# Relative attention with queries spread over heads by column multiplies, fp32 strips for Q·K, and row-wise probabilities written back as columns

## The reference

```
qx, kx, vx = split_head(x @ Wq.T), split_head(x @ Wk.T), split_head(x @ Wv.T)      # 16 heads of 8
ex   = rel_embed[ns].reshape(n, NH, HD).transpose(1, 0, 2)
srel = srel_skew(einsum('bhnd,hmd->bhnm', qx, ex))         # pad by one column, reshape, shift
qk   = (einsum('bhnd,bhmd->bhnm', qx, kx) + srel) * inv_dim
atten = softmax(qk - mask, axis=-1)                        # causal
out  = einsum('bhnm,bhmd->bhnd', atten, vx) ... @ Wp.T + bp
```

## Time and profile before

| | us |
|---|---|
| median of 3 runs | 4997.43 (4973.68 to 5001.73) |
| the profiled execution | 4969.21 |
| its span | 4967.5 |
| PE busy in the span | 4473.0 (90%), 30219 matmuls |
| DVE busy | 2379.6 (48%) |
| ACT busy | 1719.1 (35%) |
| POOL busy | 843.7 (17%) |
| mean granted PE clock | 0.912 of full speed |

### The profile page before, as it was taken

How to read it: one execution, slowest core, us unless ns; L and a number is a source line. 1 busy time by engine, 2 the same in 40 slices (tenths; PEclk the granted TensorE clock), 3 DMA queues, 4 the chain that set the end, 5 groups by cost and what they waited for, 6 DMA issues and landing times.

```text
span 4967.5 us, 76834 instructions
## 1 busy us (share of the span) xinstructions
PE 4473.0 (90%) x30219; PEld 2776.4 (56%) x30275; DVE 2379.6 (48%) x6906; ACT 1719.1 (35%) x3496; POOL 843.7 (17%) x1441
## 2 busy tenths in 40 slices
PE   7998989889898898988989889899898998989989
PEld 3556645565455654556545575455754457545575
DVE  3435634356443554435544355444554445544455
ACT  2322432325333343333433234333343333433334
POOL 2003110031100311103011040111401114011130
PEclk8989979999899998999989999899998999998989
DMA  2000000000000000000000000000000000000000
GB/s 68 1 1 1 1 6 1 1 1 1 6 1 1 1 1 6 1 1 1 1 6 1 1 1 1 6 1 1 2 1 6 1 1 2 1 3 1 1 1 3
DMA packets 19571, 17.25 MB, mean 3 GB/s; under 512 B 2462, under 2 KB 18799, under 8 KB 19183
## 3 DMA queue, kind: packets, MB, share of 16 engines
q1 hardware_dynamic: 19183, 11.99, 0.8%
HBM read 9.89 MB, written 2.10 MB: 2 GB/s over the span
## 4 chain that ended last, share of the span: by engine, by line
PE 80%; DVE 6%; POOL 6%; ACT 5%; issue 3%; DVEq 0%; ACTq 0%; POOLq 0%; SPq 0%
PE banks L984 7%; PE banks L974 7%; PE banks L988 7%; PE banks L880 7%; PE banks L908 6%; PE banks L825 6%; PE banks L920 3%; POOL work L478 3%; PE banks L865 3%; PE banks L1180 3%; PE banks L1201 2%; PE banks L1167 2%; PE banks L1074 2%; PE banks L1047 2%; PE banks L1023 2%
## 5 line engine op out<-in xcount | busy, mean ns | idle before, releaser
L1369 DVE CUSTOM_DVE_ANT_0 work<-banks,mask_row 128x512 f32<-128x512 f32 (+3 forms) x1024 | 451.6, 488 | 274.0 <-PE banks L880 270.6
L880 PE MATMUL banks<-work 32*128 32x512 f32 (+3 forms) x2048 | 526.7, 493 | 11.4 <-DVE work L1369 11.4
L908 PE MATMUL banks<-work 32*128 32x256 f32 (+3 forms) x2048 | 512.7, 504 | 20.8 <-ACT work L638 20.8
L638 ACT ACTIVATE work<-banks 128x384 f32<-128x384 f32 (+1 forms) x768 | 368.9, 526 | 441.9 <-PE banks L908 440.3
L437 POOL TENSOR_TENSOR rstd<-rstd,half 128x2 f32<-128x2 f32 x128 | 87.5, 703 | 2451.2 <-DVE moments L1297 1834.2
L654 ACT ACTIVATE work<-banks 128x512 f32<-128x512 f32 (+1 forms) x384 | 228.8, 596 | 687.6 <-PE banks L984 687.4
L1441 DVE TENSOR_TENSOR work<-work,banks 128x512 f32<-128x512 f32 (+1 forms) x384 | 263.5, 686 | 344.8 <-PE banks L988 344.5
L984 PE MATMUL banks<-xnT,wg 128*128 128x512 f32 (+1 forms) x768 | 417.8, 627 | 0.0
L988 PE MATMUL banks<-xnT,wu 128*128 128x512 f32 (+1 forms) x768 | 406.1, 611 | 0.0
L447 POOL TENSOR_SCALAR_AFFINE_SELECT work<-work 128x128 f32<-128x128 f32 (+1 forms) x768 | 252.6, 332 | 897.4 <-ACT work L638 886.1
L974 PEld LDWEIGHTS banks<-wd,work 128*128 128x128 f32 (+1 forms) x3072 | 360.6, 191 | 57.3 <-issue 57.3
(11 more groups left out here) (255 smaller groups left out, 7254.4 us busy)
## 6 DMA issues: line engine op xcount, KB each, us to landing
x_next<-in_L_attn_a_x_dram SPq DMA_DIRECT2D x8, 256.0 KB, 2.8
out_dram<-x SPq DMA_DIRECT2D x8, 256.0 KB, 2.2
wg<-in_L_ffn_Wg_dram SPq DMA_DIRECT2D x1, 1376.0 KB
wu<-in_L_ffn_Wu_dram SPq DMA_DIRECT2D x1, 1376.0 KB
wd<-in_L_ffn_Wd_dram SPq DMA_DIRECT2D x2, 512.0 KB
wk_l<-in_L_attn_a_Wk_dram SPq DMA_DIRECT2D x1, 512.0 KB, 7.8
wv_l<-in_L_attn_a_Wv_dram SPq DMA_DIRECT2D x1, 512.0 KB, 6.5
wq_l<-in_L_attn_a_Wq_dram SPq DMA_DIRECT2D x1, 512.0 KB, 7.2
```

Source lines behind the costliest of these rows:

```text
L638: eng.activation(prob4[:, G % 2, hh, C_AT[j]:C_AT[j] + C_N[j]], bank(3 + c % 3)[:, 0:C_N[j]], ACT.Exp).then_inc(s_exp, 1)
L880: m = eng.matmul(bank(k % 3)[:, col:col + N], q4[own, G, P * t:P * t + P], k4[own, G, 0:N], start=True, stop=True)
L908: m = eng.matmul(bank(3 + c % 3)[:, col:col + N], k4[own, G, P * s:P * s + P], q4[own, G, P * s:T], start=True, stop=True)
L1369: m = eng.tensor_tensor_reduce(out=summed[:, k % 2, col:col + N], in0=bank(k % 3)[:, col:col + N], in1=mask_row[:, T - N:T], scale=1.0, sc ...
```

## The change

- K and Q for the scores are no longer split and stacked. They are projected to fp32 strips (`project`, with the tables `spaced_q_r` and `padded_k_r`), four of the eight before the relative products, the other four in the first four bursts of the main part. The `spread` tables of the setup, `identb`, `mask_kq` and the mask matmuls go.
- For the relative products Q has two bf16 parts, `q_parts`. They are spread over heads by 32 multiplies of 512 columns with a column of `head_of` (26 on DVE, 6 on ACT) into `q_diag`, all before the first product. PE reads the 64 columns of a position straight from it, with a stride of 512 elements (1 KB) from head to head; before it read 64 adjacent elements.
- DVE's copies of the even blocks become multiplies with `strict`, and POOL's fill becomes MASKED.
- The main part is cut into 48 jobs (a group of four heads has 12: four with 512 columns, four with 384, four with 256 + 128), three to a burst. PE makes Q·K by rows on strips (`qk_rows`), ACT copies that to `r_rows`, PE transposes the relative scores (`shifted_rows`), DVE adds the two and takes the maximum in one instruction, ACT takes exp in place, PE transposes (`columns`), and DVE (two of three jobs) or ACT (one of three) copies them into `sc`. Values are weighed by group (`weigh_group`).

```
-                mask_q(eng, c, 0).then_inc(r_qm, 1)
+                for h in range(H - ACT_HEADS):
+                    eng.tensor_scalar(q_diag[:, 0, h, :], q_parts[:, 0, 0:T], head_of[:, h:h + 1], None, ALU.mult)
+                eng.wait_ge(r_lo, 1)
+                for h in range(H):
+                    m = eng.tensor_scalar(q_diag[:, 1, h, :], q_parts[:, 1, 0:T], head_of[:, h:h + 1], None, ALU.mult)
+                m.then_inc(r_qdv, 1)
...
                         for n, (rp, qp) in enumerate([(0, 0), (0, 1), (1, 0)]):
-                            m = eng.matmul(bank(k % 4)[:, 64 * (q % 8):64 * (q % 8) + 64],
-                                           relT[:, rp, first:first + P], q_masked[c % 2][:, qp, q % IC, :],
+                            q_now = q_diag[:, qp, :, :].rearrange("p h (t i) -> p i t h", t=NT)[:, q]
+                            m = eng.matmul(out, relT[:, rp, first:first + P], q_now,
                                            start=(n == 0), stop=(n == 2))
...
+            def qk_rows(a):
+                if a % ROWS4 == 0:
+                    eng.wait_ge(p_st, 4 * NG + 2 * G + 2)
+                if a >= BURST:
+                    eng.wait_ge(r_rows_in, a - BURST + 1)
+                for t in tiles:
+                    m = eng.matmul(bank(a % 3)[:, col:col + N], r_cols(0, G)[own, P * t:P * t + P],
+                                   r_cols(1, G)[own, 0:N], start=True, stop=True)
+            def shifted_rows(a):
+                if a >= 2:
+                    eng.wait_ge(r_max, a - 1)
+                        m = eng.transpose(bank(3 + a % 2)[:, col:col + P], sc[:, h, SLOT[(s, t)], :], ident[:, :])
+            def columns(a):
+                eng.wait_ge(r_p, a + 1)
+                if a >= 2:
+                    wait_copied(eng, a - 2)
+                    m = eng.transpose(bank(5 + a % 2)[:, col:col + P], r_rows[:, a % NROWS, col:col + P],
+                                      ident[:, :])
...
+                    m = eng.tensor_tensor_reduce(out=rows, in0=rows, in1=bank(3 + a % 2)[:, cols], scale=-1.0,
+                                                 scalar=-MASKED, op0=ALU.add, op1=ALU.min,
+                                                 accum_out=r_neg_max[:, a % NROWS, n:n + 1])
+                    m = eng.activation(v, v, ACT.Exp, scale=-1.0, bias=r_neg_max[:, a % NROWS, n:n + 1])
+                    m = copy(sc[:, h, at:at + 3 * n - 2:3, :],
+                             bk[:, col:col + n * P].rearrange("p (s i) -> p s i", s=n))
...
+            for b in range(BURSTS + 2):
+                    for a in jobs: qk_rows(a)
+                if b == 0:
+                    eng.wait_ge(r_diag, 4 * (P // IC))
+                for a in jobs:
+                        shifted_rows(a)
+                    if b >= 2:
+                        columns(a - 2 * BURST)
+                if b < 4: project(4 + b, 7)
+                if b >= 6 and b % 4 == 2: weigh_group(b // 4 - 1, range(NT))
+                if b >= 7 and b % 4 == 3: group_rows(eng, 2, b // 4 - 1, 7)
```

More of the change, by code:

```diff
@@ new lines, in exps, with copies @@
+            def exps(a):
+                tiles, hh = row_tiles(a)
+                eng.wait_ge(r_max, a + 1)
+                col = 0
+                for n, t in enumerate(tiles):
+                    v = r_rows[:, a % NROWS, col:col + (t + 1) * P]
+                    m = eng.activation(v, v, ACT.Exp, scale=-1.0, bias=r_neg_max[:, a % NROWS, n:n + 1])
+                    col += (t + 1) * P
+                m.then_inc(r_p, 1)
+            def copies(b):
+                for a in range(BURST * b, BURST * b + BURST):
+                    if not vector_copies(a):
+                        copy_columns(eng, lambda out, in_: eng.activation(out, in_, ACT.Copy), a).then_inc(r_pTa, 1)
@@ new lines, in act_rel @@
+            for b in range(BURSTS + 2):
+                if b < BURSTS:
+                    for a in range(BURST * b, BURST * b + BURST):
+                        qk_rows_in(a)
+                if b >= 2:
+                    copies(b - 2)
+                if b < 4:
+                    columns_of(4 + b, 7)
+                if 1 <= b <= BURSTS:
+                    for a in range(BURST * (b - 1), BURST * b):
+                        exps(a)
+                if b >= 7 and b % 4 == 3:
+                    group_columns(eng, 2, b // 4 - 1, 7)
@@ new lines, in weigh_group @@
+            def weigh_group(G, keys):
+                wait_copied(eng, ROWS4 * (G + 1) - 2)
+                wait_copied(eng, ROWS4 * (G + 1) - 1)
+                if G >= 1:
+                    eng.wait_ge(a_o, 2 * NG + G)
+                for s in keys:
+                    at = SLOT[(s, s)]
+                    for hh in range(G4):
+                        h = G4 * G + hh
+                        m = eng.matmul(bank(7)[32 * hh:32 * hh + 32, P * s:T],
+                                       val_row[:, s, BELOW * h:BELOW * h + 32],
+                                       sc[:, h, at:at + NT - s, :].rearrange("p b i -> p (b i)"),
+                                       start=(s == 0), stop=(s == NT - 1))
+                if keys[-1] == NT - 1:
+                    m.then_inc(s_pv, 1)
@@ L1626, in rel @@
+                for b in range(BURSTS + 2):
+                    for a in range(BURST * b, BURST * b + BURST):
+                        if b < BURSTS:
+                            row_max(a)
+                        if b >= 8 and a == BURST * b and b % 4 == 0:
+                            heads_out(2, b // 4 - 2, 7, r_rden)
+                        if b >= 2 and vector_copies(a - 2 * BURST):
+                            copy_columns(eng, eng.tensor_copy, a - 2 * BURST).then_inc(r_pTv, 1)
                 heads_out(2, NG - 1, 7, r_rden)
```

494 lines of the change are left out of this document (163 added, 331 removed).

## The result

The changed kernel is slower. Its median is 5353.7 us (4 runs, 5343.0 to 5365.3) against 4986.2 us of the kernel before on the same chip: a ratio of 1.0736, 95% interval 1.0691 to 1.0781. The profiled execution took 5365.3 us, its span 5363.6, where the one before had 4967.5. So 396 us are to be accounted for.

The account below looks back on a forecast made before the run. PE's own work was taken to set the time. 8 x (-7.3 + 1.7 - 17.1) - 5 = -187 us gave 4782 (profiled) or 4810 (median), forecast 4795; own range 4700 to 4880, full range 4690 to 5040.

Parts of the forecast that it names:

- the price of the new reading: Relative products: PE's strided reading of 64 columns taken at 30.8 ns a product, with 98 ns as high end.
- rival R2: Relative products: far reading costs about 98 ns each, PE stalls within matmuls, 27 us more a turn, 5182 us; chance 0.19.
- the range: Whole kernel: 4690 to 5040 us, taking in the forecast, R3 and R1 (half-rate reading, 57.5 ns a product, chance 0.24).
- Products without it, -7.3: Relative products, at 30.8 ns each in one piece plus 0.9 us waiting: 24.6 us against 31.9 a turn.
- POOL's wait, +1.7: After the products and first three strips: PE loses about 1.7 us a turn waiting for POOL's last chunk of selects.
- Front, no change: Before the first product: DVE's multiplies at 0.27 us each stay hidden beside the projections; other end +10 us a turn.
- R3's first half: Front: DVE's multiplies run at one element a cycle, +10 us a turn; R3 as a whole had chance 0.15.
- Main part, -17.1: Main part of relative attention: 88.7 us against 105.8 a turn, from 71.6 of PE's work plus waits and half clock.
- the waits: Main part, a turn: 3.6 us for ACT's group copy, 1.5 for the fill with ACT's table load, 4 at the end.
- Four heads weighed at once, 2.8 us: Main part, values: four heads side by side cost 2.8 us where four alone cost 9.0; the largest single gain.
- Setup, -5: Setup: POOL's memsets and selects finish ahead of PE's first transpose, transfers decide; 5 us less, once.
- the forecast's own range: Whole kernel: 4700 to 4880 us, with main-part changes between -26 and -8 us a turn.

Follow-up runs that it names:

- experiments 2: Changed kernel with a different reading pattern of PE's queries in each of 16 blocks of 48 products (wrong queries); 5141.8 us in its one run.
- experiment 7: Changed kernel with a second set of reading patterns by block of 48 products, testing what counts as a line (wrong queries); 5094.9 us in one run.
- experiment 3: Changed kernel, complete, with Q's parts laid out position by position, so each product reads 16 runs of 4 adjacent elements; 4852.6 us, ratio 0.9776 to the kernel before.
- Experiment 5: The experiment 3 version with ACT copying the finished group ahead of its burst's exps instead of behind them; 4809.4 us, ratio 0.9669 to the kernel before.
- experiment 8: The experiment 3 version with weigh_group's loops exchanged, so consecutive matmuls use the same band of 32 output columns; 5026.2 us, ratio 1.0114 to the kernel before.
- experiment 9: Kernel before, with only each product's 64 columns read at a stride of 16 elements (wrong queries); 5558.5 us, ratio 1.1163.

## Why the prediction was wrong, step by step

- **The step that failed** is the price of the new reading, "I take 30.8, the row of the instruction itself". It is 110.9 ns. The same instruction's row was no evidence, as the thing that the edit changed was what that row holds constant, the address pattern. Of the two ends I gave, 98 ns was the nearer and still too low, so rival R2 came with its mechanism (PE stands still within each matmul) and above its own time. From its 5182 us, the products' part of 86.25 us, where R2 had 76.2 (75.3 and 0.9 of waiting), makes 80 more, the main part's smaller gain 45, the output projection and the front 9, and the layers outside 51: 5366, for the measured 5365. I gave R2 0.19 and the range left it out.
- The rule of the Trainium skill, Advanced Engine Details and Errata, section on SBUF cachelines, spoke for this, and the traces agree on the 16 bytes (experiments 2 and 7). They differ on its "two hits": two bf16 elements in a line still cost 57 to 61 ns at full clock, while four are hidden (29.6); three were not seen at full clock. The measurement decides: at full clock four elements last 64 / 4 = 16 times in 29 ns, 1.8 ns, just what a line costs. I had read it as one rival among others for want of a factor.
- **Products without it, -7.3:** right. In experiment 3 they last 23.95 us with the wait for the last copy, for the forecast's 24.6.
- **POOL's wait, +1.7:** wrong, it is nothing. In experiment 3 POOL is busy only 1.03 us beyond the start of the first three strips, and PE never waits for it. The term also left out the 0.9 us that PE had just been said to wait for the last copy: 2.8 - 0.9 - 1.1 would have been 0.8.
- **Front, no change:** right. DVE's 26 multiplies lie 0.27 us apart:

```profile
466.72 2.71 DVE L1482 TENSOR_SCALAR work<-work,head_of 128x512 bf16<-128x512 bf16 x10
469.35 4.29 DVE L1485 TENSOR_SCALAR work<-work,head_of 128x512 bf16<-128x512 bf16 x16
```

  Ten start over 2.63 us, so R3's first half was not there. They do end after the projections, which leaves PE 3.5 us of waiting, because the projections ran at full clock (1.03 us) where I had reckoned with up to 2.1. That error had no effect: DVE's side came last, and it was right, ready 11.0 us after the Q product as forecast.
- **Main part, -17.1:** right in kind, -11.5 in size. Counting from start to start, PE spends 17.3 us on the strips (I said 14.4), 47.7 on 320 transposes (40), 9.2 on the values (11), 4.4 and 2.1 on projections and `group_rows` (4.2 and 1.8): 80.7, where 71.6 and 8 for half clock make 79.6. The mis-sized term is the waits, 13.6 us for 9.1:

```profile
PE banks L760 <- ACT xnT L531: 5.2, 3, 1.7
PE banks L1106 <- DVE work L1507: 3.8, 7, 1.0
PE banks L1116 <- ACT work L699: 1.7, 2, 1.5
PE banks L1116 <- DVE work L650: 1.5, 6, 0.6
```

  The wait for the group's copy is 1.73 us three times, not 1.2, and DVE's add-and-maximum (L1507) holds PE in the first bursts, which I had not counted. Experiment 5 showed what the first of these is worth: without it the main part (to the end of the last weighing, 586.6) takes 84.6 us, 21 less than before, at clock 0.98, with 75.2 us of PE's own work instead of 80.7.
- **Four heads weighed at once, 2.8 us:** 2.36. Of the 6.6 us saved on each group, 4.6 hang on the order of the bands (experiment 8).
- **Setup, -5:** -6.
- With the reading in runs the change takes 4852.6 us for the forecast 4795, inside the forecast's own range. The gain is 2.2%, about six tenths of the 187 us of the sum: what is missing is the main part's (-12 us a turn for -17), a first product 0.9 us later, and an output projection that starts at half clock.

## What to carry to other kernels

When an edit changes only an access pattern, count the 16-byte pieces that each instruction touches in order: here every piece cost PE 1.7 to 1.9 ns, so runs of four bf16 elements within 16 bytes, 1 KB apart, were free and runs of two were not. Here DVE's cheap multiplies could be kept together with such runs, by exchanging two loops of the tensor ahead of them. And where an engine waits for a small copy that stands behind long work on another engine, try the copy first: here 5.2 us of such waits in a turn's main part were gone and the part was 8.8 us shorter, as PE's clock fell less often.

## What the runs showed of the hardware that was not expected

- The time of far reading is the same at both levels of the clock: 57 ns for 32 pieces at 1.00 and at 0.50, and at 1.2 GHz two elements in a piece are nearly hidden (57 against 53 ns), while at 2.4 GHz they are not (57 against 29) and four are.
- PE counted as busy for 85.18 of 86.25 us had its clock granted at 0.50 for the whole stretch, and so had the products of experiment 9 for most of theirs. Its weight loads count as busy for 84.94 us too. A busy row is no sign of an array at work.
- Two far lines read in turn cost 62 ns, four 111 (experiment 7).
- With the same code, the two other attention layers together took 64 us more in experiment 5 than in experiment 3, and 85 more in experiment 8. The cause stays open.
